# Last attention layer with target nodes in the partitions and a softmax shift worked out ahead, in a hand-ordered four-layer pipeline

## The reference

```
xp     = h @ W_proj                                  # 512 -> 8 heads of k = 64
a_src  = xh . W_att[:, :k] ;  a_dst = xh . W_att[:, k:]
scores = leaky_relu(a_src[i] + a_dst[j] + b_att, 0.2)     # per head
scores = where(adj[i, j] > 0, scores, -1e30)
out[i] = relu(softmax_j(scores) @ xh)
```

## Time and profile before

| | us |
|---|---|
| three runs: median (lowest to highest) | 3213.99 (3212.21 to 3219.64) |
| the profiled execution, its own time | 3215.87 |
| the span in its trace, first to last instruction | 3213.9 |
| TensorE busy | 3052.3 |
| VectorE busy | 2436.3 |
| ScalarE busy | 2413.6 |
| GpSimd busy | 2116.7 |

### The profile page before, as it was taken

One profiled execution on the slowest core, in us unless ns is written; L12 is line 12 of the kernel. 1 busy time (PEld: TensorE's weight loads), 2 busy tenths in 40 slices (PEclk: granted clock), 3 DMA queues, 4 the chain that ended last, 5 costly groups with the idle time before them and its releaser, 6 DMA issues.

```text
span 3213.9 us, 77726 instructions
## 1 busy us (share of the span) xinstructions
PE 3052.3 (95%) x21776; PEld 2809.7 (87%) x21776; DVE 2436.3 (76%) x5995; ACT 2413.6 (75%) x6561; POOL 2116.7 (66%) x3236
## 2 busy tenths in 40 slices
PE   1689999999999999999999999999999999999984
PEld 0579999999999999999999999999999999999974
DVE  6477877878787787878778787887878788787752
ACT  2467778878787787877878787887878788787753
POOL 4346666766666676766767666666766677676643
PEclk6899999999999999999999999999999999999986
DMA  4112222222222222222222222222212222222211
GB/s 135 32 46 62 78 63 74 66 64 76 63 78 63 69 71 62 78 63 78 63 69 71 62 78 63 77 64 67 74 62 78 63 75 65 69 72 62 66 39 44
DMA packets 170069, 217.14 MB, mean 68 GB/s; under 512 B 34864, under 2 KB 100528, under 8 KB 169648
## 3 DMA queue, kind: packets, MB, share of 16 engines
q1 hardware_dynamic: 169648, 212.18, 22.2%
HBM read 177.55 MB, written 34.54 MB: 66 GB/s over the span
## 4 chain that ended last, share of the span: by engine, by line
PE 91%; issue 4%; DVE 1%; POOL 1%; ACT 1%; DMA 0%; POOLq 0%; DVEq 0%; ACTq 0%
PE bank_c L365 23%; PE bank_b L365 22%; PE bank_e L365 11%; PE bank_e L691 8%; PE bank_b L513 7%; PE bank_a L409 3%; PE bank_e L655 3%; PE bank_c L591 3%; PE bank_a L435 3%; PE bank_b L507 2%; PE bank_b L358 2%; PE bank_e L358 2%; PE bank_a L396 0%; PE bank_a L422 0%; PE bank_c L579 0%
## 5 line engine op out<-in xcount | busy, mean ns | idle before, releaser
L365 PE MATMUL bank_b<-w_hi,hT_hi 128*128 128x344 f32 x1536 | 470.1, 360 | 7.2 <-DVE hT_lo L1215 6.7
L365 PE MATMUL bank_c<-w_hi,g_hi 128*128 128x258 f32 x2048 | 413.2, 283 | 2.4 <-DVE x L1171 2.4
L365 PE MATMUL bank_c<-w_lo,g_hi 128*128 128x258 f32 x2048 | 413.2, 283 | 0.0
L365 PE MATMUL bank_b<-w_lo,hT_hi 128*128 128x344 f32 x1536 | 410.2, 321 | 0.0
L1474 POOL TENSOR_TENSOR eE<-eE,nmE 128x512 f32<-128x512 f32 x256 | 266.2, 1040 | 178.0 <-DVE nmE L1289 177.0
L1467 POOL TENSOR_TENSOR eE<-t_all_L,mask 128x512 f32<-128x512 f32 x256 | 349.0, 1384 | 32.3 <-DMA t_all_L<-t_dram_L 31.5
L1455 POOL TENSOR_TENSOR g_lo<-g,g_hi 128x512 fp32r<-128x512 f32 x128 | 193.9, 1515 | 262.0 <-ACT g_hi L901 262.0
L365 PE MATMUL bank_c<-w_hi,g_lo 128*128 128x258 f32 x2048 | 363.8, 289 | 0.7
L940 ACT ACTIVATE eE<-eE,st 128x128 f32<-128x128 f32 x1024 | 326.1, 391 | 40.5 <-POOL eE L1467 40.4
L365 PE MATMUL bank_b<-w_hi,hT_lo 128*128 128x344 f32 x1536 | 347.2, 321 | 0.0
L365 PEld LDWEIGHTS bank_b<-w_hi,hT_hi 128*128 128x128 f32 x1536 | 277.7, 189 | 75.0 <-issue 67.1
(11 more groups left out here) (136 smaller groups left out, 8785.5 us busy)
## 6 DMA issues: line engine op xcount, KB each, us to landing
t_all_L<-t_dram_L SPq DMA_DIRECT2D x128, 512.0 KB, 3.9
x_in<-in_x SPq DMA_DIRECT2D x128, 256.0 KB, 2.5
t_all_L1a<-t_dram_L1a SPq DMA_DIRECT2D x128, 256.0 KB, 4.3
out<-out_sb SPq DMA_DIRECT2D x128, 256.0 KB, 4.2
t_all_L<-t_dram_L SPq DMA_DIRECT2D x256, 64.0 KB, 2.9
adj_in<-in_adj SPq DMA_DIRECT2D x128, 64.0 KB, 2.6
t_dram_L1a<-t_rows_L1a SPq DMA_DIRECT2D x512, 0.5 KB
t_all_L1b<-t_dram_L1b SPq DMA_DIRECT2D x128, 64.0 KB, 2.8
```

What stands on the lines that cost most here:

```text
L365: last = mm(bank[:, 0:width], a[:, c * P:(c + 1) * P], w[:, c, b * width:(b + 1) * width], start=(first and c == chunks[0] and n == 0), st ...
```

## The change

**The scores stand the other way round.** In the last layer the target node j now lies in the partition and the source i in the free dimension, so that the exponentials come out as the product wants them. The 8 transposes of `pE`, the two copies to `pTE`, and the tiles `pE`, `pTE`, `rE` are gone; `product_half_L3` reads `eT`.

**The softmax shift has to be known ahead.** A maximum over j would now run across partitions. So VectorE works it out beforehand with sources in the partitions: `most_L3` adds the mask to the spread target scores and takes the maximum, one instruction per head (8 of 128 columns, each with a read of its result), in place on `t_all_L3`. As the leaky relu is monotone, `most_leaky_L3` adds the source score to that maximum and applies the leaky relu to the sum, on 8 columns. `rows_shift_L3` transposes source scores and shifts together, `send_shift_L3` writes them to DRAM with 4 DMAs, and `spread_shift_L3` spreads both (16 rows of 128, 1 MB) into `shift_all`. GpSimd then adds the mask to the first 8 rows (`masked_L3`), ScalarE adds the target score, now the bias (`tc3`), and GpSimd subtracts the other 8 rows (`shift_L3`), which are a whole operand where a broadcast column stood. The mask itself is needed turned: `turn_mask_L3` on TensorE and `copy_mask_L3` on ScalarE, 128x128, once per graph.

**Smaller edits.** VectorE writes the result into `out_sb` directly. `x3` has 4 slots, `xa` two. The three semaphores of `scale_and_bias` became one that counts to 3. **All five lists have a new order and new skews**: the input is loaded in step 0 instead of 1, L1a starts at skew 2 to 3 instead of 4 to 5, L1b ends at 5 instead of 6 to 7, L3's projection stands at 9, its softmax at 10 and its product at 11; store stays at 12.

```diff
+            def send_shift_L3(g):
+                if g.live:
+                    sp.wait_ge(sem("L3_shift_rows"), g.made())
+                    sp.wait_ge(sem("L3_shift_spread"), 16 * g.made(2))
+                    for b in range(P // Q):
+                        sp.dma_start(shift_dram[g.slot(2), :, b * Q:(b + 1) * Q],
+                                     shift_rows[b * Q:b * Q + 2 * H3, :]).then_inc(sem("L3_shift_sent"), 16)
+
+            def spread_shift_L3(g):
+                if g.live:
+                    sp.wait_ge(sem("L3_shift_sent"), 16 * (P // Q) * g.made())
+                    sp.wait_ge(sem("L3_shifted0"), g.made(1))
+                    sp.wait_ge(sem("L3_shifted1"), g.made(1))
...
+                    src = shift_dram[g.slot(2):g.slot(2) + 1, :, :]
+                    sp.dma_start(shift_all[:], src.to_broadcast([P, 2 * H3, P])).then_inc(sem("L3_shift_spread"), 16)
...
-            def turn_exp_half_L3(g, i):
-                for k in range(HB):
-                    last = nc.tensor.transpose(bank_e[:, i, k * P:(k + 1) * P], pE[:, i * HB + k, :], ident[:])
-                last.then_inc(sem(f"L3_turned{i}"), 1)
...
+                    mm(bank_a[:, 0:P], mask[:, g.slot(MR), :], identb[:], start=True, stop=True)\
+                        .then_inc(sem("flat_turned"), 1)
...
-                    last = mm(bank_e[:, i, k * KA:k * KA + NMIN], pTE[:, head, :],
-                              xa[:, head * KA:head * KA + NMIN], start=True, stop=True)
+                    last = mm(bank_e[:, i, k * KA:k * KA + NMIN], eT[:, head, :],
+                              xa[:, g.slot(VR), head * KA:head * KA + NMIN], start=True, stop=True)
...
-                    activation(pE[:, half, :], eE[:, half, :], ACT.Exp).then_inc(sem(f"L3_exp{i}"), 1)
-
-            def pT_L3(i, g):
...
+                    activation(eT[:, half, :], eT[:, half, :], ACT.Exp).then_inc(sem(f"L3_exp{i}"), 1)
...
             def most_L3(i, g):
                 if g.live:
-                    dve.wait_ge(sem(f"L3_leaky{i}"), g.made())
-                    dve.wait_ge(sem(f"L3_shifted{i}"), g.made(1))
-                    half = slice(i * HB, (i + 1) * HB)
-                    nc.vector.tensor_reduce(nmE[:, half], eE[:, half, :], AX_X, ALU.max, negate=True)\
-                        .then_inc(sem(f"L3_max{i}"), 1)
+                    dve.wait_ge(sem("L3_spread"), 16 * g.made())
+                    dve.wait_ge(sem("mask_made"), g.made())
+                    dve.wait_ge(sem("L3_most_leaky"), g.made(1))
+                    for k in range(i * HB, (i + 1) * HB):
+                        last = nc.vector.tensor_tensor_reduce(t_all["L3"][:, k, :], t_all["L3"][:, k, :],
+                                                              mask[:, g.slot(MR), :], 1.0, -3.0e38, ALU.add, ALU.max,
+                                                              most3[:, k:k + 1])
+                    last.then_inc(sem(f"L3_most{i}"), 1)
...
+                    tt(most3[:], most3[:], shift_cols[:, 0:H3], ALU.add).then_inc(sem("L3_most_sum"), 1)
+                    dve.wait_ge(sem("L3_most_sum"), g.made())
+                    stt(shift_cols[:, H3:2 * H3], most3[:], SLOPE, most3[:], ALU.mult, ALU.max)\
+                        .then_inc(sem("L3_most_leaky"), 1)
...
             def shift_L3(i, g):
                 if g.live:
                     half = slice(i * HB, (i + 1) * HB)
-                    pool.wait_ge(sem(f"L3_max{i}"), g.made())
-                    nm = nmE[:, half].rearrange("p (h a) -> p h a", a=1).to_broadcast([P, HB, P])
-                    tt(eE[:, half, :], eE[:, half, :], nm, ALU.add).then_inc(sem(f"L3_shifted{i}"), 1)
+                    pool.wait_ge(sem(f"L3_leaky{i}"), g.made())
+                    tt(eT[:, half, :], eT[:, half, :], shift_all[:, H3 + i * HB:H3 + (i + 1) * HB, :], ALU.subtract)\
+                        .then_inc(sem(f"L3_shifted{i}"), 1)
...
             for step in range(G + SKEW):
                 t = Turn(G, step)
-                product_L1b(t, t.graph(7))
...
+                turn_prob_L1a(t, t.graph(4))
```

455 lines of the change are left out of this document (231 added, 224 removed).

## The result

The changed kernel takes 3160.61 us (median of 4 runs, 3155.09 to 3162.35) against 3214.03 (3212.21 to 3219.64): 0.9828 of the time before, 95% interval 0.981 to 0.9846. It is faster by some 53 us, where 144 were predicted (3070). The profiled execution has a span of 3160.6 us.

The account below looks back on a forecast made before the run. TensorE's list was taken to bound the middle, latencies both ends: filling 224, 120 steps of 22.66 (2719) and draining 124 make 3067, with some 3 us of stray waits 3070 us against 3214; range 3040 to 3160.

Parts of the forecast that it names:

- I expect one or two stops of about 1 us a step, which fit into 3.0: VectorE beside GpSimd on their shared path: stops of about 1 us fit into the 3.0 us left per step.
- 19.6 in the sum: VectorE's work per step after the change, 19.6 us against a step of 22.66.
- TensorE's list: TensorE's step without the 8 transposes (0.87 us) and with one mask turning (0.06): 22.66 us instead of 23.465.
- rival (a): VectorE becomes the bound in part through stopped products or late hT_lo: step 23.1, 3120 us; chance 0.15.
- Even 7.8 leaves slack: The shift's new 1 MB spread lands in 5.0 us, bounds 3.9 and 7.8, and even 7.8 is early enough.
- where that queue has idle time: SyncE's 5 more issues a step fall ahead of L1a's and L3's sends, in idle time between landings.
- The filling: First steps: L1a's first turning at 92, then steps of 18 and 21 us, so step 11 begins at 224.
- The draining: Last steps: 7 of 16 us, plus about 12 us to the last store, 124 in all.
- rival (b): Two hops through DRAM lengthen the last layer's way, so draining gives nothing: 3115 us; chance 0.07.
- (c): Slower: VectorE and GpSimd take turns as a rule; added stops exceed 3.9 us, step 25.3, 3385 us; chance 0.10.
- (d): TensorE's list is shorter but product_L3 waits for exponentials in every step: about 3175 to 3214 us; chance 0.05.
- the 16.8: GpSimd's work per step with the shift's whole second operand: 16.8 us of 22.66.

Follow-up runs that it names:

- e11: e2 plus eight two-input products on unused values, placed ahead of the last layer's reciprocal where VectorE stands idle: 3073.87 us.
- e12: e2 plus eight two-input products on unused values, at the two places where the changed kernel has its own: 3266.03 us.
- e3: Changed kernel with half of the shift's spread (512 KB), the 8 rows of the shift itself left out: 3103.64 us.
- e9: Changed kernel with VectorE's reciprocal for L1a's probabilities ahead of the second half's products: 3243.72 us.
- e17: e13 with the spreads of L0's and L1b's targets both ahead of the shift's sends on SyncE: 3109.04 us.
- e13: Changed kernel with L1b's row turned ahead of the first half's four products, SyncE's order unchanged: 3150.44 us.
- e6: Changed kernel with eight plain one-input maxima of 128 columns in place of the eight products with the mask: 3075.74 us.
- e7: Kernel before without turning the last layer's exponentials and without ScalarE's two copies of them: 3139.26 us.
- e5: Changed kernel with SyncE's loads of a graph issued behind the shift's 1 MB spread: 3148.00 us.
- e2: Changed kernel with two plain maxima of 512 columns, no mask, in place of the eight products: 3068.69 us.
- e15: e2 with the last half of the third weights staged in step 2, as in e4: 3066.16 us.
- e4: Changed kernel with the last half of the third weights staged by SyncE in step 2 instead of 3: 3155.98 us.
- e16: Changed kernel with all eight products behind L1b's row, and L0's and L1b's spreads ahead of the shift's sends: 3185.79 us.
- e18: e15 with the spreads of L0's and L1b's targets both ahead of the shift's sends: 3068.31 us.

## Why the prediction was wrong, point by point

**The step that failed: "I expect one or two stops of about 1 us a step, which fit into 3.0."** The sizes were right: VectorE is busy for 665.42/800 x 23.15 = 19.3 us a step (19.6 in the sum), and the stops are 1.2 us a step in all. That they fit was wrong: the step grew by 0.80 us over TensorE's list (23.15 for 22.35). I compared VectorE's idle time over the whole step with the added work, as if idle time could be filled anywhere. But TensorE's step hangs on a round over VectorE, SyncE, a spread and GpSimd's ordered list, and the products were put just where VectorE is on it. e11 and e12 show that the place counts: the same work is 5 us at one place and 197 at the other. e3, e9 and e17 against e13 show the round's members one by one: a shorter spread gives 57 us back, a longer way to L1b's row costs 83, an earlier spread gives 41. e6 shows that it is the two-input form (85 of 92 us) and not the eight instructions. It came nearest to rival (a), and close in size (a step of 23.1), though VectorE was not the bound; I had given it 0.15, on the ground that TensorE had not waited before when the engines met. It had not, since its own list was longer: in e7, where that list is shorter (and two copies of ScalarE are gone), it waits for the same probabilities in every step.

**"Even 7.8 leaves slack"** (the 1 MB spread) was right for that spread and left out its neighbour. It landed in 7.1 us, within the bounds, and from 320 to 2960 us GpSimd never waited for it (L1493). But the spread of L1b's targets beside it went from 2.8 to 4.9 us, and that one is on the round. With both small spreads ahead the large one took 4.7, near the 5.0 that I had worked out. The pages of before, after (two rows) and e17:
```profile
t_all_L1b<-t_dram_L1b SPq DMA_DIRECT2D x128, 64.0 KB, 2.8
```
```profile
t_all_L1b<-t_dram_L1b SPq DMA_DIRECT2D x128, 64.0 KB, 4.9
```
```profile
shift_all<-shift_dram SPq DMA_DIRECT2D x128, 1024.0 KB, 7.1
```
```profile
shift_all<-shift_dram SPq DMA_DIRECT2D x128, 1024.0 KB, 4.7
```

**SyncE's issues "where that queue has idle time"**: four sends of the shift (1.78 us on the median, at times over 3) stand ahead of L1b's spread. e17 against e13, 41 us for SyncE's order alone, shows it as a term; e5 points the same way with 13 us. The term was missing.

**TensorE's list** was sized 22.66 and is 22.35 (e2, e6, e15 in most steps). The direction was right, and the list by itself would have given 37 us more. By itself, in the old order, the shorter list is worth 78 us (e7), more than the whole change: all the rest of it together costs time. But e7 gives only 0.54 of the 0.87 us in the old order, where the wait for GpSimd's probabilities comes next; which part of the rest belongs to the new order was not tried.

**The filling** (224 against 252) was right in its mechanism only. The first turning came at 105 instead of 92. TensorE waited for the last weights there:
```profile
PE bank_b L389 <- POOL w_lo L1399: 8.8, 1, 8.8
```
Behind SyncE's wait for a row stood the last load of the weights; e4 took 3.6 of it off. From there seven steps took 21.0 each, not 18 to 21: TensorE works for 130.50 of 147 us there, while its work per step was put at 16. Without the products it is the same (e2: 146.4), so they are not its cause. What else lies in it was not tried.

**The draining** came close to the forecast, 131 us for 124: from product to product (L698), the last four steps took 15.7 each, in place of 20.4, but the first three behind the mark took 19.8, and the end behind the last product 8.6 instead of 12. The chain of waits of the kernel after:
```profile
3097.49 1.16 POOL eT L1493
...
3113.51 1.17 POOL eT L1493
...
3130.22 1.17 POOL eT L1493
```
So rival (b) is out. (c) needed stops of over 3.9 us a step (its 347 + 120 x 25.3 is 3383, not 3385). (d) is out too: TensorE has no row of waits for the exponentials from 320 to 2960 us, and e2 lets the same order run at TensorE's pace. GpSimd's 608.56/800 x 23.15 = 17.6 a step is above the 16.8, but e2, without the products, has 614.13/800 x 22.41 = 17.2: about half of the excess is of the new order (below).

**The rule of the Trainium skill** on VectorE's two-input instructions and GpSimd (page "SBUF — State Buffer", section "Who interferes with whom") holds here: by it e6 had to come out near e2, since one input leaves the path to GpSimd, and it did (3075.74 against 3068.69). The prediction had the rule but counted the stops only against VectorE's idle time.

**Sum of the corrections**: 3067, less 37 for the list, plus 96 for 0.80 us of waits in 120 steps, 28 for filling and 7 for draining, is 3161. The measured time lies beside the end of the range (3160), and that says nothing for the forecast: its picture of a TensorE that never waits did not hold.

## What to carry to other kernels

Before idle time of an engine is counted as room, find the round on which its neighbours hang: follow one step back over engines, queues and transfers until it closes on itself, and ask whether the new instruction stands on it. If it does, its time and its stops count, however idle the engine is over the step (197 us here); a place off the round cost almost nothing (5 us). When TensorE's list is shortened, the next round has to be timed before the gain is booked, and a DMA-issuing queue with a wait in it is a member like any engine.

## What the hardware showed that I had not expected

- GpSimd's one-column operations are stopped too. Before, `rs` of L1386 took 264 to 268 ns in the steady part; after (L1413, 442 of them) 264 to 1374, with the same median of 265. It is not the change's products that do this: in e2, which has none of them, the same operation took 265 to 1373, with a mean of 446 against 451. All 108 of them that took over 0.7 us lie beside one of VectorE's two-input products of 512 columns (L1111), which the new order brought there. The eight products lengthen others: the making of the loop mask (L1441) has a median of 560 ns, in e2 429.
- Spreads issued one right behind another stretched each other: 1 MB landed in 7.1 us (median) with two spreads of 64 KB issued 0.9 and 0.5 us ahead of it, and in 4.7 in e16, e17 and e18, where the four sends stand between; the spread of L1b took 4.9 instead of 2.8 (2.9 in e17). The loads are not the cause: e5 moves them behind, and the 1 MB took 7.2.
- The four sends of the shift (2 KB each) hold SyncE for 1.78 us in one step and for 3.30 in another, both right behind loads of 320 KB. Why is open: with the loads behind them (e5) 7% of the steps still took over 2.5 us, and in e2, with the loads where they were, only 1%, against 21% in the changed kernel.
- A reciprocal of 0.18 us moved ahead made the kernel 83 us slower than the changed one (e9). GpSimd's long operation then started earlier, and the product of 1.12 us beside it came on the way to L1b's row.
